# A fused transformer block on one core: output projection of the second attention from fp32 to fp16 halves, a second copy of its normalised rows, and a new list of steps

## What is computed

```
x = x + attn_a(layernorm(x))      # linear attention, 16 heads of 64, running sums over 2048 rows, then @ Wo + bo
x = x + ffn(layernorm(x))         # int8-quantised rows @ int8-quantised rhs, scales put back
x = x + attn_b(layernorm(x))      # x @ q_w.T, k_w.T, v_w.T, rotary turn, ranks 16, gate, decaying state -> Y
                                  #   hres = x_norm + Y @ out_w.T + out_b ; layernorm(hres) * ln_g + ln_b
x = x + ffn(layernorm(x))         # the same rhs
```

## Time and profile before

| what | us |
|---|---|
| median of 3 runs (lowest, highest) | 3149.44 (3147.72, 3150.87) |
| the profiled execution, its own time | 3152.03 |
| its span, first to last instruction | 3150.2 |
| PE busy | 3027.0, 96% of the span |
| DVE busy | 2457.6, 78% |
| POOL busy, ACT busy | 1028.1, 734.0 |
| mean granted TensorE clock | 0.983 |

### The profile page before, as it was taken

One profiled execution on the slowest core, in us unless ns is written; L12 is line 12 of the kernel. 1 busy time (PEld: TensorE's weight loads), 2 busy tenths in 40 slices (PEclk: granted clock), 3 DMA queues, 4 the chain that ended last, 5 costly groups with the idle time before them and its releaser, 6 DMA issues.

```text
span 3150.2 us, 126598 instructions
## 1 busy us (share of the span) xinstructions
PE 3027.0 (96%) x54932; PEld 2288.7 (73%) x54932; DVE 2457.6 (78%) x5410; ACT 734.0 (23%) x1357; POOL 1028.1 (33%) x1398
## 2 busy tenths in 40 slices
PE   3699999999999999999999999999999999999995
PEld 3477777777777777777777777777777777777763
DVE  7777787787787887787787778778778778778774
ACT  2222221222222222222122122222222222222211
POOL 2023333333333333333333333333333333333332
PEclk9799999999999999999999999999999999999997
DMA  5222222222222222222222222222222222222220
GB/s 176 62 40 50 42 45 50 42 45 51 41 45 51 41 49 47 44 47 49 44 48 45 45 47 45 51 41 45 51 41 47 49 42 48 49 46 45 48 41 20
DMA packets 384395, 153.89 MB, mean 49 GB/s; under 512 B 352801, under 2 KB 361633, under 8 KB 383905
## 3 DMA queue, kind: packets, MB, share of 16 engines
q1 hardware_dynamic: 383904, 146.02, 23.4%
HBM read 45.29 MB, written 16.78 MB: 20 GB/s over the span
## 4 chain that ended last, share of the span: by engine, by line
PE 94%; DVE 3%; issue 1%; DMA 1%; ACT 0%; POOL 0%; POOLq 0%; SPq 0%; DVEq 0%; ACTq 0%
PE bank L726 22%; PE bank L727 21%; PE bank L728 21%; PE bank L1020 7%; PE bank L899 3%; PE bank L808 3%; PE bank L852 3%; PE bank L684 3%; PE bank L972 2%; PE bank L871 2%; PE bank L826 2%; PE bank L995 2%; PE bank L982 1%; DVE absmax L1163 1%; PE bank L1008 1%
## 5 line engine op out<-in xcount | busy, mean ns | idle before, releaser
L726 PE MATMUL bank<-xaT,wq_hi 128*128 128x128 f16 x2048 | 362.5, 221 | 4.5 <-DVE absall L1173 4.5
L726 PE MATMUL bank<-xbT,wb 128*128 128x128 f16 x2048 | 350.8, 220 | 13.3 <-DMA xbT<-work 13.3
L727 PE MATMUL bank<-xaT,wq_hi 128*128 128x128 f16 x2048 | 361.1, 221 | 0.0
L728 PE MATMUL bank<-xaT,wq_lo 128*128 128x128 f16 x2048 | 361.0, 221 | 0.0
L726 PE MATMUL bank<-xaT,wk_hi 128*128 128x128 f16 x2048 | 358.5, 220 | 0.0
L727 PE MATMUL bank<-xaT,wk_hi 128*128 128x128 f16 x2048 | 358.4, 220 | 0.0
L728 PE MATMUL bank<-xaT,wk_lo 128*128 128x128 f16 x2048 | 358.4, 220 | 0.0
L727 PE MATMUL bank<-xbT,wb 128*128 128x128 f16 x2048 | 350.8, 220 | 0.0
L728 PE MATMUL bank<-xbT,wb 128*128 128x128 f16 x2048 | 350.7, 220 | 0.0
L646 POOL TENSOR_TENSOR work<-work 128x512 f32<-128x512 f32 x128 | 162.3, 1268 | 421.4 <-DVE work L1418 421.4
L1306 DVE TENSOR_SCALAR work<-bank,eps_q 128x256 f32<-128x256 f32 x256 | 122.9, 480 | 175.8 <-PE bank L728 172.1
(11 more groups left out here) (210 smaller groups left out, 8438.7 us busy)
## 6 DMA issues: line engine op xcount, KB each, us to landing
xin<-in_L_attn_a_x SPq DMA_DIRECT2D x64, 256.0 KB, 2.6
out<-xf SPq DMA_DIRECT2D x64, 256.0 KB, 2.1
table<-in_tables SPq DMA_DIRECT2D x64, 192.5 KB, 2.5
work<-in_L_attn_a_Wq SPq DMA_DIRECT2D x1, 2048.0 KB, 8.2
work<-in_L_attn_a_Wk SPq DMA_DIRECT2D x1, 2048.0 KB, 12.6
wb<-in_L_attn_a_Wv SPq DMA_DIRECT2D x1, 2048.0 KB, 17.3
work<-in_L_attn_a_Wo SPq DMA_DIRECT2D x1, 2048.0 KB, 8.5
work<-work SPq DMA_TRANSPOSE x128, 3.6
```

What stands on the lines that cost most here:

```text
L726: nc.tensor.matmul(o, a[0], b[0], start=first, stop=False)
L727: nc.tensor.matmul(o, a[0], b[1], start=False, stop=False)
L728: return nc.tensor.matmul(o, a[1], b[0], start=False, stop=last)
```

## The change

1. `out` multiplies fp16 halves: `wout` becomes a pair of fp16 tiles, prepared in the start as the other weights are (`load out`, `max out`, `all out`, `scale out`, `hi out`, `lo out`), and the early load of the fp32 tile goes. For Y the scale is found anew in each chunk: `y_m` (DVE) takes the largest absolute value of each partition of `yT`, `y_r` (PE) transposes that column, `y_s` (DVE) takes the largest over all, and makes a power of two and its inverse, `y_h` (ACT) writes the upper half, `y_l` (DVE) the lower. `out_e` multiplies the inverse back in.
2. `xnb` has two copies, taken in turn; `nb_ap` waits for `x3_ready` two chunks back. `xf1` has one copy in place of two, so `nf1_ap` waits for the store of the chunk just before.
3. A new `ORDER` (119 entries) with new `BANK`, `LATE`, `BORROWED` and `COUNTS`. Several waits of a step are joined where they concern the same bank (`all_filled`, `take_behind`). The list is turned so that it ends with `out` of lag 4; `mm1`, `out_e` and what follows it have lag 5.

PE's order in a full slot after: `gb qb vb so0 so1 oa0 oa1 ob0 ob1 u0 u1 kb qk0 qk1 qk2 mm0 kr mm1 qk3 qr kT wo0 sb ys wo1 kt1 ub yb v0 y_r kt0 s0 s1 v1 out`. DVE's: `s0_e out_e xTa_l no_st s1_e no_ap gb_e no_f nf1_st qb_e nf1_ap o0_e nf1_q kb_e o1_e aT0_l qb_l kb_l u0_e qk1_e aT1_l kr_e mm1_e mm0_e qk0_e qk2_e u1_e qr_e nb_st qk3_e sb_e1 sb_e0 nb_ap wo_e ub_e nf0_st y_m xTb_l y_s nf0_ap na_st y_l nf0_q na_ap`.

```diff
-ORDER = [("no_rs", 4), ("wo0", 2), ("no_ap", 4), ("no_f", 4), ("nb_ap", 3), ("xTb_h", 3), ("nf1_st", 4), ("wo1", 2),
...
-         ("out", 3), ("out_e", 3), ("no_st", 3), ("ld_t", 2), ("ub_a", 3), ("u0_e", 1)]
+ORDER = [("s0_e", 2), ("x2l", 4), ("out_e", 5), ("xTa_h", 1), ("xTa_l", 1), ("gb", 4), ("no_st", 5), ("qb", 4),
...
+         ("wo_e", 2), ("ld_t", 3), ("kt1", 1), ("ub", 4), ("yb", 4), ("ld_x", 0), ("y_e", 4), ("ub_e", 4),
+         ("v0", 1), ("nf0_st", 2), ("xTb_h", 3), ("st_o", 5), ("y_m", 4), ("kt1_e", 1), ("y_r", 4),
+         ("xTb_l", 3), ("xTb_t", 3), ("v0_e", 1), ("kt0", 1), ("nf0_rs", 2), ("y_s", 4), ("nf0_ap", 2),
+         ("na_st", 0), ("kt0_e", 1), ("y_h", 4), ("na_rs", 0), ("y_l", 4), ("nf0_q", 2), ("rnd0", 2), ("s0", 1),
+         ("s1", 1), ("v1", 1), ("na_ap", 0), ("out", 4)]
...
+    (3, "oa1"): ("scale rk", "hi rk", "max rq", "all rq", "load out"),
+    (3, "gb_s"): ("lo rk", "scale rq", "hi rq"),
+    (3, "kb"): ("lo rq",),
+    (3, "qT1_t"): ("max out", "all out"),
+    (3, "qk2_e"): ("scale out", "hi out"),
+    (3, "ld_t"): ("lo out",),
...
+    def take_behind(self, units, read):
+
+        last = {}
+        for u in units:
+            last[BANK[u]] = max(last.get(BANK[u], (0, -10 ** 9)), self.uses(u), key=lambda n: n[1])
+        for u, back in read:
+            if self.exists(back):
+                per, const = self.uses(u, back)
+                last[BANK[u]] = max(last.get(BANK[u], (0, -10 ** 9)), (per, const + 1), key=lambda n: n[1])
+        for b, n in last.items():
+            self.wait(self.empty[b], n)
+        return [(self.ps[BANK[u]], self.full[BANK[u]]) for u in units]
...
-        wout = sb("wout", [P, KD, D])
+        wout = (sb("wout_hi", [P, KD, D], F16), sb("wout_lo", [P, KD, D], F16))
...
-        xf1 = sb("xf1", [P, 2, D])
+        xf1 = sb("xf1", [P, D])
...
-        xnb = sb("xnb", [P, D])
+        xnb = sb("xnb", [P, 2, D])
...
-            sp.dma_start(wout[:, :, :], out_w.rearrange("(k p) n -> p k n", p=P)).then_inc(s_wout, 16)
...
-                    pair = [c.take(f"s{g}a"), c.take(f"s{g}b")]
-                    c.done(f"qk{2 * g}")
-                    c.done(f"qk{2 * g + 1}")
+                    pair = c.take_behind((f"s{g}a", f"s{g}b"), ((f"qk{2 * g}", 0), (f"qk{2 * g + 1}", 0)))
...
+            def y_r(c):
+
+                bank, f = c.take("ym")
+                c.wait(y_reduced, c.count())
+                nc.tensor.transpose(bank[:, 0:P], y_max[:, :].to_broadcast([P, P]), ident[:, :]).then_inc(f, 1)
+
             def out_(c):
                 bank, f = c.take("out")
-                c.done("y0")
-                c.done("y1")
-                if c.per == 0 and c.j == 0:
-                    pe.wait_ge(s_wout, 16)
+                c.wait(y_halved, c.count())
+                need(c, "out")
                 for k in range(KD):
-                    last = nc.tensor.matmul(bank[:, :], yT[:, k, :], wout[:, k, :], start=k == 0, stop=k == KD - 1)
+                    last = three_pass(bank[:, :], (y_split[:, 0, k, :], y_split[:, 1, k, :]), w_part(wout, k, slice(0, D)),
+                                      k == 0, k == KD - 1)
...
+            def y_h(c):
+                c.wait(y_scaled, c.count())
+                c.filled("sb3")
+                nc.scalar.activation(y_split[:, 0, :, :], yT, ACT.Copy, scale=y_scale[:, :]).then_inc(y_hi, 1)
...
             def nf1_ap(c):
-                c.wait(out_free[c.par], c.half(2, each=16))
-                normalise("f1", c, xwb[:, c.par, :], xf1[:, c.par, :])
+                c.wait(out_free, c.count(1, each=16))
+                normalise("f1", c, xwb[:, c.par, :], xf1[:, :])
...
             def nb_ap(c):
-                c.wait(x3_ready, c.count(1))
-                normalise("b", c, xwb[:, c.par, :], xnb[:, :])
+                c.wait(x3_ready, c.count(2))
+                normalise("b", c, xwb[:, c.par, :], xnb[:, c.par, :])
...
+            def y_m(c):
+                c.done("y0")
+                c.done("y1")
+                nc.vector.tensor_reduce(y_max[:, :], yT.rearrange("p k t -> p (k t)"), AX_X, ALU.max,
+                                        apply_absolute_value=True).then_inc(y_reduced, 1)
+
+            def y_s(c):
+
+                bank, e = c.read("ym")
+                nc.vector.tensor_reduce(y_all[:, :], bank[:, 0:P], AX_X, ALU.max).then_inc(e, 1)
+                c.done("ym")
+                nc.vector.tensor_scalar(y_small[:, :], y_all[:, :], 2.0 ** -80, 2.0 ** -12, ALU.max, ALU.mult)\
+                    .then_inc(y_bounded, 1)
+                c.wait(y_bounded, c.count())
+                nc.vector.tensor_scalar(y_exponent[:, :].bitcast(U32), y_small[:, :].bitcast(U32), 0x7F800000, None,
+                                        ALU.bitwise_and).then_inc(y_power, 1)
+                c.wait(y_power, c.count())
+                nc.vector.tensor_scalar(y_scale[:, :].bitcast(U32), y_exponent[:, :].bitcast(U32), 0x7F800000, None,
+                                        ALU.bitwise_xor).then_inc(y_scaled, 1)
+                nc.vector.tensor_scalar(y_unscale[:, c.par:c.par + 1], y_exponent[:, :], unscale[:, SOUT:SOUT + 1], 0.5,
+                                        ALU.mult, ALU.mult)
+
+            def y_l(c):
+                c.wait(y_scaled, c.count())
+                c.wait(y_hi, c.count())
+                nc.vector.scalar_tensor_tensor(y_split[:, 1, :, :], yT, y_scale[:, :], y_split[:, 0, :, :], ALU.mult,
+                                               ALU.subtract).then_inc(y_halved, 1)
+
             def out_e(c):
                 bank, e = c.read("out")
                 c.wait(xn_bias, c.count())
-                nc.vector.tensor_tensor(xnb[:, :], bank[:, :], xnb[:, :], ALU.add).then_inc(e, 1)
+                nc.vector.scalar_tensor_tensor(xnb[:, c.par, :], bank[:, :], y_unscale[:, c.par:c.par + 1], xnb[:, c.par, :],
+                                               ALU.mult, ALU.add).then_inc(e, 1)
```

More of the change, by code:

```diff
@@ L79 @@
 MAX_LAG = max(LAG.values())
[L82 to L85, removed]
+BANK = {"v0": 5, "v1": 4, "qk0": 7, "qk1": 1, "qk2": 5, "qk3": 4, "kt0": 7, "s0a": 0, "s0b": 1, "o0a": 1, "o0b": 5,
+        "u0": 4, "kt1": 4, "s1a": 2, "s1b": 3, "o1a": 2, "o1b": 3, "u1": 0, "wo": 3, "mm0": 6, "qb": 7, "kb": 6,
+        "vb": 0, "gb": 6, "qr": 1, "kr": 2, "sb0": 6, "sb1": 7, "sb2": 5, "sb3": 0, "y0": 2, "y1": 1, "ub": 0,
+        "out": 5, "ym": 6, "mm1": 3}
 BANKS = 8
 TAKES = {"s0a": "s0", "s0b": "s0", "s1a": "s1", "s1b": "s1", "o0a": "so0", "o0b": "so0", "o1a": "so1", "o1b": "so1",
-         "wo": "wo0", "y0": "sb", "y1": "sb", "sb0": "sb", "sb1": "sb", "sb2": "sb", "sb3": "sb"}
+         "wo": "wo0", "ym": "y_r", "y0": "sb", "y1": "sb", "sb0": "sb", "sb1": "sb", "sb2": "sb", "sb3": "sb"}
 SETUP_UNITS = 3
@@ L103 @@
 LATE = {
[L104 to L120, removed]
[5 rows of a table removed]
-}
[L128 to L139, removed]
+    (1, "u0"): ("load o",),
+    (1, "mm1_a"): ("max o",),
+    (1, "wo0"): ("turn decay",),
+    (1, "sb_e0"): ("all o", "keep decay"),
+    (1, "nf0_st"): ("scale o", "hi o"),
+    (1, "y_s"): ("lo o", "load rhs", "load bk"),
+    (2, "v1_e"): ("max rhs", "all rhs"),
+    (2, "oa1"): ("columns of rhs", "rows of rhs"),
+    (2, "nf1_st"): ("scale rhs",),
+    (2, "gb_s"): ("max bk", "all bk"),
+    (2, "qk1"): ("scale bk", "hi bk"),
+    (2, "aT1_l"): ("round rhs", "load bq"),
[12 rows of a table added]
+    (3, "qT1_t"): ("max out", "all out"),
+    (3, "qk2_e"): ("scale out", "hi out"),
+    (3, "ld_t"): ("lo out",),
+}
+TAKEN = ("q", "k", "v", "o", "rhs", "bk", "bq", "g", "bv", "rk", "rq", "out")
+BORROWED = {"decay": (1, "wo0", 0),
+            "o": (1, "sb_e0", 2),
+            "rhs": (2, "v1_e", 7),
+            "rhs rows": (2, "oa1", 0),
+            "bk": (2, "gb_s", 6),
+            "bq": (2, "qk3_e", 7),
+            "g": (2, "yb", 0),
+            "bv": (2, "nf0_q", 7),
+            "rk": (3, "v1_e", 7),
+            "rq": (3, "oa1", 6),
+            "out": (3, "qT1_t", 2)}
 def borrowed_before(bank, slot, place):
@@ L367, in hybrid_kernel @@
         block16 = xwb[:, 1, 256:384].rearrange("p (h i) -> p h i", h=HALF_H)
-        rhs_max = xf1[:, 0, :]
-        rhs_inverse = xf1[:, 1, :]
+        rhs_max = xnb[:, 0, :]
+        rhs_inverse = xnb[:, 1, :]
         rhs_cols = sb("rhs_cols", [P, KD])
@@ L414, in hybrid_kernel @@
         table_loaded = sem("table_loaded")
-        out_free = [sem(f"out_free{p}") for p in range(2)]
+        out_free = sem("out_free")
         loaded = {n: sem(f"loaded_{n}") for n in TAKEN}
@@ L506, in st_o @@
                 c.wait(out_ready, c.count())
-                sp.dma_start(at(out, c), xf1[:, c.par, :]).then_inc(out_free[c.par], 16)
+                sp.dma_start(at(out, c), xf1[:, :]).then_inc(out_free, 16)
             def transpose(n, to, src):
@@ L549, in _ @@
                  "load g": lambda: load("g", g_w, "bk"), "load bv": lambda: load("bv", v_w, "bq"),
```

(19 more changed lines are left out.)

101 lines of the change are left out of this document (53 added, 48 removed), and 59 rows, old and new, of tables (COUNTS, LATE, ORDER).

## The result

The changed kernel takes **3169.3 us** (median of 4 runs, 3166.7 to 3170.7) beside 3149.9 of the kernel before on the same chip: a ratio of 1.0061, interval 1.0044 to 1.0079. It is slower by 0.6%, where 1.5% faster was forecast. The profiled execution is that of 3166.7 us; its span is 3164.9. The medians of the runs further on leave out one execution of joint_behind_run (3236.6 us) and one of fp32_out (4421.5 us) that had a much lower granted clock than the others.

A forecast was written before the change was run, and what follows sets the result against it. PE was taken to bound the slots, DVE and latency the start. Even slots −47, start +12 and end −13 us sum to −48, so 3149.4 becomes a forecast of 3101 us, −1.5%, range 3080 to 3127.

The forecast's parts named there:

- The even slots: 60 full slots between start and end: `out` −0.90 us, `y_r` +0.11, net −0.79 each, −47 us in all.
- The y chain: Steps `y_m` to `y_l` ahead of `out`: hidden, with 1.2 us to spare before `y_r` and 1.1 before `out`.
- Rivals 1 and 2: DVE's port shared with POOL makes `y_l` late, 3131 us, 10%; the chain through y sets the slot, 3185, 5%.
- Rival 5: In `out`: it does not get shorter, as the halves' matmuls cannot follow at 0.216 us; under 1%.
- The joint: Where the loop's turns meet: cost may fall to zero (−10 us) or grow (+10 us); no change taken.
- The start: Up to the first full slot: 5.5 us of added DVE work plus 7 for one more chunk, +12 us.
- DVE's share: In the start, DVE's 7 us of the extra chunk's work, taken as nearer than PE's some 15.
- The end: Last three slots with an `out`: together −13 us, from −25 to +3; slots of 37 and 35.5 us named.
- The tail: Behind the last `out_e`: its 17.9 us stay.
- the slower side: Whole kernel slower by more than 6 us, chance 0.05, given to the chain through y setting the slot.

The follow-up runs named there:

- joint_behind_run: Changed kernel with the loop's joint turned to just ahead of `kb`, behind the row of small matmuls, same order of work; 3161.4 us, ratio 1.0043.
- fp32_out: Changed kernel with the output projection in fp32 again, without the y steps and the preparation of `out_w`'s halves; 3129.8 us, ratio 0.9941.
- pad_128: Changed kernel with 128 increments of an unused semaphore at the head of PE's program; 3096.8 us, ratio 0.9835.
- before_pad_192: Kernel before the change with 192 increments of an unused semaphore ahead of PE's queue; 3162.3 us, ratio 1.0039.
- pad_128_spread: Changed kernel with 128 unused semaphore increments, 44 and 84 placed where PE waits for the second and third weights' maxima; 3091.8 us, ratio 0.9819.
- split_u: Changed kernel with `u0` and `u1` moved behind `kb`, so full-size matmuls stand between `ob1` and `u0`; 3162.7 us, ratio 1.0039.
- pad_192: Changed kernel with 192 increments of an unused semaphore at the head of PE's program; 3141.7 us, ratio 0.9978.
- before_pad_64: Kernel before the change with 64 increments of an unused semaphore ahead of PE's queue; 3198.5 us, ratio 1.0158.
- long_start: Changed kernel with slots 12 to 31 written out too, so the loop has 16 turns instead of 26; 3102.6 us, ratio 0.9852.
- pad_64: Changed kernel with 64 increments of an unused semaphore at the head of PE's program; 3100.5 us, ratio 0.9844.

## Why the prediction was wrong

Step by step, by its own order.

- **The even slots**: the terms were right. `out` 2.59 us, `y_r` 0.11 (1563.49 to 1563.60), so −0.79 a slot. At a place without gaps the new list with fp32 takes 46.56 a slot and with halves 45.72 (the means of fp32_out's and pad_128's two slots): −0.84.
- **The y chain**: right. `y_m` was to have 1.2 us to spare and has 1.2; `y_l` was to end 1.1 us before `out` and ends 1.5 before. Rivals 1 and 2 did not come about: PE has no wait for L1531 or L1509 in the middle. Rival 5 did not either.
- **The joint: here it failed.** "The cost may fall to zero (−10 us over 26 turns) or grow; the trace has no such order. The nearest row for an upper end is the same 0.4 again, +10 us. I take no change." The order of work around the joint was looked at, but not that PE's instructions themselves have to be brought in, in blocks whose ends fall where the length of all code in front puts them; no term of the sum had that. The change lengthened and reshuffled PE's start, and so moved them. That term measured 2826.7 − 2758.8 = +68 us against the forecast, and 2826.7 − 2745.7 = +81 against the same list at a good place; 66 of it are the gaps in `u`. Most of the rest, 12.9 us, stands as busy time (2756.49 against 2743.63): the last matmul ahead of a gap runs out alone, and its record of some 0.27 us, where in the row one starts every 0.02, comes to an estimated 0.25 for each of the 54 gaps. The 0.4 us that the prediction took for the joint's cost was in part the place too: at a good place the two slots differ by 0.16 us with the new list, and in before_pad_192 by 0.18 (46.72, 46.54) with the old.
- **The start**: +5.2 where +12 was taken. PE absorbed more of the extra chunk than "DVE's share". **The end**: −11.0 where −13 was taken. The slots took 40.2, 35.1 and 34.7 against 37, 35.5 and 35.3: the first, still with parts of the first attention, was the one mis-sized. **The tail** stayed.
- **No rival held this case**; the slower side was given to a wait for another engine, and the warning that was in the rows, "issue" in the chain and small groups stretched behind the joint in the earlier trace rows, was priced as a constant of the joint.

At a good place of the code the forecast of 3101 stands beside 3096.8 (pad_128) and 3091.8 (pad_128_spread). That nearness is in part luck: in pad_128 the 60 slots are 13 us shorter than forecast (2745.7 against 2758.8), while the last three are 3 longer and the padding's start comes on top. By parts: list and second copy −19 us (fp32_out, against 3148.7 of the kernel before in its batch), the halves a further −33 to −38, the place up to +77 (3169.3 to 3091.8). The halves save 51 us in the 60 slots (2745.7 against 2796.9) and give some 9 back in the last three (111.0 against 102.3), where the maximum, scale and halves of Y stand open.

Left open: when PE asks for its next block, and so why an end of a block costs 0.5 to 2.2 us at some instructions of the row and nothing at others (in pad_128 a packet begins inside the row, at 1510.50, and there is no gap). So the good place has to be found by trying. A list that does not depend on the place, with full-size matmuls strewn among the small ones everywhere, was not tried; split_u, which did it at one spot, did not help where its code stood.

## What to carry to other kernels

Where the trace shows PE's instructions fetched anew in every turn of a loop (14 or 15 packets here), two kernels are compared fairly only at several places of their code: shift the program by a quarter, a half and three quarters of a block (64, 128, 192 instructions here) and compare the best of each, before a difference under some 3% is put down to the edit. An idle time of PE that the profile puts to "issue", at the same instruction in every turn and inside a row of small matmuls, is the sign; a few instructions without effect, placed where PE waits anyway, can be worth more than the edit.

## What was not expected of the hardware

- The same program, moved in steps of 64 instructions, ran in 3096.8 to 3186.9 us, and the kernel before in 3149.9 to 3231.1. Up to 23 us of these lie in the start, with the padding; the loop's slots alone differ by 1.55 us of 45.72, 3.4%, and those of the kernel before by 1.4 of 46.63. With 256 instructions the gaps came back to the same place.
- PE uses up a block of 256 instructions in some 2.4 us in the row of small matmuls (two instructions for each of 192 in 3.6 us). Most gaps stand in or right behind such rows: in `u` (L904), behind it (pad_192), in `oa` and `ob` of the kernel before (L852), and three transposes behind them (before_pad_64, L684). PE goes on 2.2 to 3.2 us after the packet that it needs began.
- Written-out code is not spared: the slots ahead of the loop in long_start, which have no jump, lose up to 1.75 us each in two to four of every five or six.
- The jump back at the joint is no measure of the loss: in the trace it lasts 0.46 us on PE (median) in the kernels before and after, and 1.3 to 3.6 us in long_start, fp32_out, pad_128 and pad_64, whose loops show hardly a gap. The Trainium skill, "Advanced Engine Details and Errata", § Control Flow Timing, has about 108 ns for a compare-and-branch; on PE only the last one of each loop comes near it, which is not taken and lasts 0.09 us.
- An increment of a semaphore at the head of PE's program takes 0.16 us: with 192 of them PE's first matmul starts at 30.35 us, with 256 at 40.37. The first matmul waited until 14.9 us anyway, and later waits take up a part, so that 128 moved the first `out_e` by 8.1 us and 256 by 22.7.
